# Two preparing stages move into the programs of the attentions behind them

## The reference

```
x = L0_attn_a_hidden_states                     # (8, 512, 128)
x = x + slot_attention(layernorm(x))
x = x + experts(layernorm(x))                   # base_w, lora_A, lora_B, router, top 2 of 8
x = x + polar_attention(layernorm(x))           # 16 heads of 8
x = x + experts(layernorm(x))
x = x + distance_attention(layernorm(x))
x = x + squared_relu_ffn(layernorm(x))
x = x + gated_attention(layernorm(x))
x = x + squared_relu_ffn(layernorm(x))
```

```
q_embed = stack([q_mag * cos(qp), q_mag * sin(qp)]);  k_embed = stack([k_mag * cos(kp), k_mag * sin(kp)])
attn = softmax(einsum(q_embed, k_embed) / D ** 0.5);  out = attn @ v @ wo.T
```

```
G = -(j - P) ** 2 * 2.0 / Z ** 2
probs = softmax(q @ k / sqrt(D) + G);  out = probs @ v @ wo + bo
```

## Time and profile before

| what | value |
|---|---|
| median of 3 runs | 1889.18 us |
| the profiled execution | 1887.09 us |
| its span in the profile | 1885.3 us |
| TensorE (PE) busy | 1622.4 us, 86% |
| VectorE (DVE) busy | 1251.8 us, 66% |
| ScalarE (ACT) busy | 1294.3 us, 69% |
| GpSimd (POOL) busy | 349.0 us, 19% |
| mean granted clock of TensorE | 0.92 |

### The profile page before, as it was taken

The page is one execution under the profiler, slowest core; times in us unless marked ns, Lnnn a source line. Parts: engine busy times, 40 slices in busy tenths (PEclk is TensorE's granted clock), DMA queues, the critical chain, the costliest instruction groups (busy, mean ns, idle before and its releaser), DMA issues. The chain is left out here.

```text
span 1885.3 us, 39080 instructions
## 1 busy us (share of the span) xinstructions
PE 1622.4 (86%) x14558; PEld 779.6 (41%) x14558; DVE 1251.8 (66%) x2538; ACT 1294.3 (69%) x2190; POOL 349.0 (19%) x634
## 2 busy tenths in 40 slices
PE   7899976762999999976789999777764999999988
PEld 4666754640233333346533333344430333333356
DVE  4777776896999999946410010145656999999833
ACT  4556542882688888864579999656662888888863
POOL 3424221441000000014300000023321000000153
PEclk9999995985899999997989999899975999999999
DMA  4000000046222222200131111002233112212101
GB/s 120 1 1 1 1 1 1 10 139 170 64 76 73 81 73 73 67 2 4 40 92 60 58 58 58 3 17 60 82 90 90 56 56 61 63 56 63 35 7 40
DMA packets 114624, 99.04 MB, mean 53 GB/s; under 512 B 25866, under 2 KB 104516, under 8 KB 114436
## 3 DMA queue, kind: packets, MB, share of 16 engines
q1 hardware_dynamic: 112636, 95.61, 17.4%
q10 hardware_dynamic: 1800, 0.92, 0.2%
HBM read 64.34 MB, written 32.11 MB: 51 GB/s over the span
## 5 line engine op out<-in xcount | busy, mean ns | idle before, releaser
L1551 ACT ACTIVATE m_probs<-m_psum 128x512 f32<-128x512 f32 (+1 forms) x768 | 513.7, 758 | 120.1 <-PE m_psum L1459 118.7
L1551 ACT ACTIVATE e_probs<-e_psum 128x512 f32<-128x512 f32 x512 | 277.3, 597 | 82.9 <-PE e_psum L1459 81.6
L1594 DVE TENSOR_REDUCE a_minus_max<-e_psum 128x1 f32<-128x512 f32 x512 | 317.1, 682 | 12.7 <-PE e_psum L1468 5.3
L1594 DVE TENSOR_REDUCE a_minus_max<-m_psum 128x1 f32<-128x512 f32 x512 | 317.0, 682 | 11.7 <-PE m_psum L1468 4.5
L1459 PE MATMUL m_psum<-m_q_stack,m_k_stack 114*32 114x512 bf16 (+1 forms) x4096 | 296.7, 385 | 10.5 <-DMA m_k_stack<-n_parts 8.4
L1479 PE MATMUL m_psum<-m_probs,m_v_ones 128*32 128x512 f32 x2048 | 272.7, 601 | 2.2 <-ACT m_probs L1551 1.4
L1459 PEld LDWEIGHTS m_psum<-m_q_stack,m_k_stack 114*32 114x32 bf16 (+1 forms) x4096 | 105.2, 96 | 211.4 <-issue 113.3
L1459 PE MATMUL e_psum<-e_q_stack,e_k_stack 126*32 126x512 bf16 x2048 | 160.2, 385 | 2.1 <-ACT e_probs L1551 2.1
L1468 PE MATMUL m_psum<-m_k_stack,m_q_stack 48*128 48x512 bf16 x512 | 112.5, 401 | 35.0 <-DMA m_k_stack<-polar_k 34.3
L1468 PE MATMUL e_psum<-e_k_stack,e_q_stack 60*128 60x512 bf16 x512 | 112.6, 401 | 31.6 <-DMA e_q_stack<-gate_parts 31.0
L1479 PE MATMUL e_psum<-e_probs,e_v_ones 128*32 128x512 f32 x1024 | 135.3, 596 | 0.9 <-ACT e_probs L1551 0.8
(11 more groups left out here) (394 smaller groups left out, 2751.3 us busy)
## 6 DMA issues: line engine op xcount, KB each, us to landing
polar_q<-d_p_q_parts SPq DMA_DIRECT2D x24, 256.0 KB, 3.0
polar_k<-d_p_k_parts SPq DMA_DIRECT2D x24, 256.0 KB, 3.1
m_q_stack<-polar_q SPq DMA_DIRECT2D x64, 96.0 KB
m_q_stack<-dist_parts SPq DMA_DIRECT2D x192, 32.0 KB
m_k_stack<-dist_parts SPq DMA_DIRECT2D x192, 32.0 KB
gate_parts<-d_p_curve_parts SPq DMA_DIRECT2D x24, 256.0 KB, 3.0
m_k_stack<-polar_k SPq DMA_DIRECT2D x62, 96.0 KB
e_q_stack<-gate_parts SPq DMA_DIRECT2D x64, 72.0 KB
```

The source lines that it names most:

```text
L1551: act.activation(self.buf.probs[(NT * m + c) % self.buf.PROBS][:, self.WIDE * part:self.WIDE * (part + 1), :], self.ps_s[i % self.PAIRS], ...
L1594: dve.tensor_reduce(self.minus_max[n % 2][:, k:k + 1], ps[:, :], AX.X, ALU.max, negate=True).then_inc(self.bank_free, 1)
```

## The change

The polar stage becomes the class `PolarPhase` and the gated stage the class `GatedPhase`; their steps are called from the streams of `middle_group` and `last_group`, ahead of the attention, and the two programs of their own are gone. So that both fit, the stage's memory lies in the attention's: a helper `Pieces` cuts tensors out of others. Of the polar stage, the normalisation and the experts lie in the buffers `ctxT`, `v_ones` and `probs`, soft and mag in stacks 2 and 3, and the embeddings in `ctx`; the parts lie in a tensor `late`, which the stage behind the attention uses again. The PSUM banks are those of the group. Where an engine takes over a piece, it waits for `early_done` or `all_done` of the stage, and at a bank for `bank_done`.

The attention's beginning is spread over the stage's last steps. Stacks 0 and 1 are filled in polar steps 6 and 7 and loaded behind the stores of blocks 1 and 2, and stacks 2 and 3 are filled behind the stage and loaded behind its last store. In the gated stage stacks 0 and 1 are filled and loaded in steps 7 and 8, and stacks 2 and 3 in step 10. The key stacks of the polar attention are filled by GpSimd. TensorE goes on with the attention's step 0 behind its last stage step (`TAIL`), and VectorE takes the maxima of unit 0 in four chunks (`vector_chunk`) in the last stage steps. In the gated stage the temporaries ez, th and dist lie in the curve tensor itself.

The diff, cut to its core:

```diff
+class Pieces:
...
+    def alloc_sbuf_tensor(self, name, shape, dtype):
+        size = math.prod(shape[1:]) * (2 if dtype == BF16 else 4) // 4
+        room = -(-size // 8) * 8
+        i = next(i for i, region in enumerate(self.regions) if self.used[i] + room <= region.shape[1])
+        piece = self.regions[i][0:shape[0], self.used[i]:self.used[i] + size]
+        self.used[i] += room
+        if dtype != F32:
+            piece = piece.bitcast(dtype)
+        names = "abcd"[:len(shape) - 1]
+        return piece.rearrange(f"p ({' '.join(names)}) -> p {' '.join(names)}", **dict(zip(names, shape[1:])))
...
-        self.soft = [sb(f"{tag}_soft{u}", [P, 2, T], F32) for u in range(2)]
-        self.mag = [sb(f"{tag}_mag{u}", [P, 2, T], F32) for u in range(2)]
-        self.embed = [[sb(f"{tag}_{n}_embed{u}", [P, 2, T], F32) for u in range(2)] for n in "qk"]
+        self.soft = [middle.alloc_sbuf_tensor(f"{tag}_soft{u}", [P, 2, T], F32) for u in range(2)]
+        self.mag = [middle.alloc_sbuf_tensor(f"{tag}_mag{u}", [P, 2, T], F32) for u in range(2)]
+        self.embed = [[context.alloc_sbuf_tensor(f"{tag}_{n}_embed{u}", [P, 2, T], F32) for u in range(2)] for n in "qk"]
...
-        act.activation(self.ez[b % 2][:, :], self.banks.of("z")[:, :], ACT.Exp, scale=-1.0).then_inc(self.ez_ready, 1)
+        wait_ge(act, self.c_split.rest_ready, b - 1)
+        steep = self.curve[b % 2][:, 2, :]
+        act.activation(steep, self.banks.of("z")[:, :], ACT.Exp, scale=-1.0).then_inc(self.ez_ready, 1)
         act.wait_ge(self.ez_ready, b + 1)
         act.wait_ge(self.consts_ready, 1)
-        wait_ge(act, self.c_split.rest_ready, b - 1)
-        act.activation(self.curve[b % 2][:, 2, :], self.ez[b % 2][:, :], ACT.Square, bias=self.consts[:, 1:2], scale=self.SHARP).then_inc(self.steep_ready, 1)
+        act.activation(steep, steep, ACT.Square, bias=self.consts[:, 1:2], scale=self.SHARP).then_inc(self.steep_ready, 1)
...
-        curve, dist = self.curve[b % 2], self.dist[b % 2]
+        curve = self.curve[b % 2]
...
-        dve.tensor_tensor(curve[:, 1, :], dist[:, :], curve[:, 2, :], ALU.mult).then_inc(self.slope_ready, 1)
+        dve.tensor_tensor(curve[:, 1, :], curve[:, 0, :], curve[:, 2, :], ALU.mult).then_inc(self.slope_ready, 1)
         dve.wait_ge(self.slope_ready, b + 1)
-        dve.tensor_tensor(curve[:, 0, :], dist[:, :], curve[:, 1, :], ALU.mult).then_inc(self.curve_ready, 1)
+        dve.tensor_tensor(curve[:, 0, :], curve[:, 0, :], curve[:, 1, :], ALU.mult).then_inc(self.curve_ready, 1)
...
+    def early_done(self, eng):
+        for i in range(2):
+            eng.wait_ge(self.prep.embed_ready[i], NB)
+        eng.wait_ge(self.prep.v_done, NB)
+        eng.wait_ge(self.prep.v_ready, NB)
...
+    def early_done(self, eng):
+        eng.wait_ge(self.prep.p_done, NB)
+        eng.wait_ge(self.prep.v_done, NB)
+        eng.wait_ge(self.prep.k_split.lo_ready, NB)
...
+    def late_pieces(self):
+        return [t[:, :] for t in self.ctxT] + [t[:, :, :, :].rearrange("p t h c -> p (t h c)") for t in self.v_ones] \
+            + [t[:, :, :].rearrange("p h t -> p (h t)") for t in self.probs]
+
+    def stack_pieces(self):
+        return [t[u][:, :, :].rearrange("p h t -> p (h t)").bitcast(F32) for u in range(2, self.SLOTS) for t in (self.q_stack, self.k_stack)]
...
-    def load(self, sp, n, queries=True, keys=True):
+    def load(self, sp, n):
         b, g = divmod(n, NG)
         sp.wait_ge(self.filled[g], self.FILLS)
         wait_ge(sp, self.scores_done, self.UNITS * (n - self.buf.SLOTS + 1))
-        parts = self.loads(b, g, self.buf.q_stack[g], self.buf.k_stack[g])
-        for wanted, part in zip((queries, keys), parts):
-            if wanted:
-                for src, dst in part:
-                    sp.dma_start(dst, src).then_inc(self.loaded[g], 16)
+        for part in self.loads(b, g, self.buf.q_stack[g], self.buf.k_stack[g]):
+            for src, dst in part:
+                sp.dma_start(dst, src).then_inc(self.loaded[g], 16)
 
...
-    def sync(self, sp, skip=0, keys_from=0):
-
+    def sync(self, sp, skip):
+
+        if self.with_max:
+            for n in range(2, skip):
+                self.max_to_stack(sp, n - 2)
         for n in range(skip, self.N):
-            if self.before is not None and n % NG == 0:
+            if n % NG == 0:
                 self.before.parts_stored(sp, n // NG)
-            self.load(sp, n, keys=n >= keys_from)
-            if self.with_max and n >= 2:
+            self.load(sp, n)
+            if self.with_max:
...
+    def fill_key(self, eng, u):
+        k = self.buf.k_stack[u]
+        if self.fixed is not None:
+            last = eng.tensor_copy(k[0:self.rows, 0:GH:2, :], self.fixed[0:self.rows, 0, :].unsqueeze(1).to_broadcast([self.rows, GH // 2, T]))
+        elif self.with_max:
+            eng.wait_ge(self.filled[u], 1)
+            eng.memset(k[32:64, :, :].bitcast(F32), 0.0).then_inc(self.zeroed, 1)
+            eng.wait_ge(self.zeroed, u + 1)
+            last = eng.memset(k[96:self.rows, :, :].bitcast(F32), self.ONES)
...
+    def vector_chunk(self, dve, s, c):
+        if self.with_max and s < self.N:
+            for k in range(4 * c, 4 * c + 4):
+                self.reduce_tile(dve, s, k)
...
+        late = nc.alloc_sbuf_tensor("m_late", [P, 15744], F32)
+        context = Pieces(nc, [sv.ctx[:, :, :].rearrange("p t d -> p (t d)")])
+        polar = PolarPhase(nc, sv, "d3", Pieces(nc, buf.late_pieces()), Pieces(nc, buf.stack_pieces()), context, Pieces(nc, [late[:, :]]), psum)
+        first = Attention(nc, sv, "a3", buf, psum, ((0, 1, 2), 3, (4, 5, 6, 7)), l0b_loads(sv), first=6 * DH, second=6 * DH, before=polar)
...
+        TAIL = NB + 4
+        FILLS = range(6, 8)
 
         with nc.Block() as block:
             @block.sync
             def _(sp):
-                first.sync(sp, keys_from=1)
+                for b in range(NB):
+                    polar.store(sp, b)
+                    if b == 1:
+                        polar.parts_stored(sp, 0)
+                    if 1 <= b <= 2:
+                        first.load(sp, b - 1)
+                first.load(sp, 2)
+                first.load(sp, 3)
+                first.sync(sp, skip=NG)
...
-                first.fill_queries(pool)
+                for s in range(polar.STEPS):
+                    polar.gpsimd(pool, s)
+                    if s in FILLS:
+                        first.fill_query(pool, s - FILLS[0])
+                        first.fill_key(pool, s - FILLS[0])
+                polar.early_done(pool)
+                for u in range(2, NG):
+                    first.fill_query(pool, u)
+                    first.fill_key(pool, u)
                 buf.set_up(pool)
...
-                for s in range(N + first.LAG):
+                polar.vector_start(dve)
+                for s in range(polar.STEPS):
+                    polar.vector(dve, s)
+                    if s == TAIL + 2:
+                        first.zero(dve)
+                    if s >= TAIL + 2 and s - TAIL - 2 < NT:
+                        first.vector_chunk(dve, 0, s - TAIL - 2)
+                polar.early_done(dve)
+                for s in range(1, N + first.LAG):
...
+        late = nc.alloc_sbuf_tensor("e_late", [P, 16128], F32)
+        early = Pieces(nc, buf.late_pieces()[0:4] + buf.stack_pieces() + [sv.pope_table[:, :, :].rearrange("p c t -> p (c t)")] + buf.late_pieces()[4:7])
+        gated = GatedPhase(nc, sv, "d7", sv.l1a_wo[:, :], early, Pieces(nc, [late[:, :]]), psum)
...
+        TAIL = NB + 2
+        FILLS = {NB - 1: (0,), NB: (1,), NB + 2: (2, 3)}
 
         with nc.Block() as block:
             @block.sync
             def _(sp):
-                attention.sync(sp, keys_from=1)
+                for s in range(gated.STEPS):
+                    gated.store(sp, s)
+                    if s == NB - 1:
+                        gated.parts_stored(sp, 0)
+                    for u in FILLS.get(s, ()):
+                        attention.load(sp, u)
+                attention.sync(sp, skip=NG)
                 for b in range(NB):
...
-                for s in range(N + attention.LAG):
+                gated.vector_start(dve)
+                for s in range(gated.STEPS):
+                    gated.vector(dve, s)
+                    if s == NB + 2:
+                        gated.early_done(dve)
+                    for u in FILLS.get(s, ()):
+                        attention.fill_key(dve, u)
+                    if s == TAIL:
+                        attention.zero(dve)
+                        attention.vector_chunk(dve, 0, 0)
+                        attention.vector_chunk(dve, 0, 1)
+                for c in range(2, NT):
+                    attention.vector_chunk(dve, 0, c)
+                for s in range(1, N + attention.LAG):
                     attention.vector(dve, s)
+                    if s == N:
...
-    polar_phase(nc, sv, "d3")
     middle_group(nc, sv)
```

(1 more changed line is left out.)

694 lines of the change are left out of this document (362 added, 332 removed).

## The result

The changed kernel takes 1861.11 us, the median of 4 runs (1858.68 to 1862.63), against 1888.76 us of the kernel before (4 runs beside it, 1886.36 to 1891.96): ratio 0.9848, 95% interval 0.983 to 0.9865. The forecast was 1863.3. The profiled execution is the one of 1858.68 us, span 1856.8.

The account below looks back on a forecast made before the run. TensorE bounds the dense attentions; the two seams before them, last held by SyncE's queue, can shrink. 12.6 + 14.3 - 1.0 = 25.9 us off 1887.09 gives 1861.2; with 2.09 for the median, 1863.3 us; range 1854 to 1875.

Parts of the forecast that it names:

- The queue was last at both seams: Before both attentions, SyncE's queue sets step 2, later than VectorE: by 5.7 us after polar, 1.6 after gated.
- rival A: Queue not last; both steps 2 start by VectorE's path, 34.2 us earlier in all, 1855.0 us; chance 0.14.
- VectorE's path: Step 2 if VectorE alone set it: 461.4 after polar (gain 18.3 us), 1442.2 after gated (gain 15.9).
- Seam 1, SyncE's path: Polar stage to its attention: last store, loads 2 and 3, then rows; step 2 at 467.1, gain 12.6 us.
- Seam 2: Gated stage to its attention: curve stores and loads, then rows; step 2 at 1443.8 by the queue, gain 14.3 us.
- The fills: Stack fills inside polar steps 6, 7 and gated steps 7, 8: 1.0 us taken as cost, between 0 and 8.
- The chunks "earn nothing as such": Unit 0's maxima among the last polar operations: VectorE has no idle time to hide them; the gain is its 18.8 us waiting.
- Rival D: Slower: TensorE's clock stays at 0.5 on into the attention; 1902 us after four such steps; chance 0.04.
- Rival B: About half the gain: steady polar and gated steps get longer; gain 12 us, 1877 us; chance 0.16.
- Rival C: Loads or fills released so late that a wait of equal length replaces the seam; gain within 4 us, 1889; chance 0.04.
- the forecast's own range: Whole kernel: the row landing at both ends and 0 to 8 us for the fills, about 1859 to 1872 us.
- The row's landing: Landing of unit 0's row DMA before step 2: 1.7 us, bounds 0 to 3.7, within 3.3 for the rows.

Follow-up runs that it names:

- e1: Changed kernel with the rows of unit 0's maxima sent ahead of load 3 (polar seam) and ahead of the last curve store (gated seam): 1855.54 us.
- e5: Changed kernel with unit 0's rows sent earlier on SyncE's queue and all chunks of its maxima behind the stages' last steps: 1857.66 us.
- The repeated trace: The changed kernel run again with no edit, in two later sessions: 1868.48 and 1863.43 us.
- e8: Changed kernel with each stack load issuing the DMAs of the keys ahead of those of the queries: 1868.84 us.
- e2: Changed kernel with all four chunks of unit 0's maxima behind each stage's last step, SyncE's order kept: 1860.73 us.
- e4: Changed kernel with the polar stage back in a program of its own, only the gated stage joined to its attention: 1871.21 us.
- e7: Changed kernel with chunks of unit 0's maxima in VectorE's waits, the others last, and rows sent behind load 2: 1852.17 us, again 1849.44.

## Why the prediction was right, and where its sum was off

**The mechanism held.** The queue was last at both seams, as the forecast said against rival A, and e1 shows it by moving two DMAs. VectorE's path, the second limit, lay where the sum had it: 31.9 us behind the last magnitude, 31.88 in e5; at seam 2, 1442.2 - 1410.24 = 32.0, measured 31.1. Rival A is refuted as a description of this kernel; its price was right to within 1 us per seam, and e5 reaches it.

**Seam 1, SyncE's path: 12.6 predicted, 10.3 measured.** This term was 2.3 too large. The repeated trace has its last magnitude at 429.54, as before, so its times compare directly with the sum. SyncE and TensorE in it:

```profile
451.81 1.85 SPq L940 DMA_DIRECT2D polar_k<-m_late  x3
453.70 3.71 SPq L1464 DMA_DIRECT2D m_q_stack<-polar_q  x6
457.46 2.78 SPq L1464 DMA_DIRECT2D m_k_stack<-polar_k  x6
...
465.91 0.43 SPq L1469 DMA_DIRECT2D a_max_dram<-a_max_rows  x1
467.79 0.24 SPq L1471 DMA_DIRECT2D m_q_stack<-a_max_dram  x1
...
469.34 1.04 PE L1532 MATMUL m_psum<-m_q_stack,m_k_stack 114*32 114x512 bf16 x8 [7.90 <-issue]
```

The last polar_k store ends at 453.66 instead of 452.9 (0.8, the polar_q store ahead of it holds the queue); load 2 ends 6.6 us later instead of 5.5 (1.1, the six DMAs behind the stores, e8); load 3 takes 0.2 more; L1469 to L1471 1.9 instead of 1.4 (0.5; with a free queue it was 1.37); the landing of the row load 1.3 behind the end of its issue instead of 1.7 (-0.4). Together 2.2 in this trace. The prices were taken where the queue was free, or where no stores stood just ahead, and were used for a full queue behind stores.

**Seam 2: 14.3 predicted, 13.3 measured.** Counted from the last curves, the queue came to the rows 1.0 us late: the stores of block 6's curve parts began 0.5 later than before, load 2 took 6.2 instead of 5.85 behind them, load 3 6.0. The rows themselves took the 3.3 of the sum (1426.22 to 1429.51). VectorE's path was 0.8 shorter than mine, because the two fills of the key stack took 1.29 us there and not 2.53, as three in a row had made me expect; 0.4 of the 1.2 us went into a longer wait for ScalarE ahead of them (5.27 instead of 4.83).

**The fills: 1.0 taken, 0 measured in the polar half.** The polar stage is as long as before. For the gated half there are only the traces at equal clock above, so its part of the 1.0 stays open. The six late fills ran from 437.00 to 443 us, four of them wholly or partly beside VectorE's two-input operations (L634 and L449), and took 0.94 to 0.96 each, against 3.62 / 4 = 0.9 in the earlier trace rows; GpSimd in the profile after:

```profile
437.00 0.95 POOL L1491 MEMSET m_q_stack<- 114x1024 f32 x1 [21.18 <-DVE ctx L621]
438.01 0.94 POOL L1630 MEMSET m_k_stack<- 32x1024 f32 x1
...
442.03 0.95 POOL L1632 MEMSET m_k_stack<- 18x1024 f32 x1
```

A memset, which reads nothing, is not held up there, while the operation that reads (L216 in the earlier trace rows, L241 above) takes 1.04 to 1.11 us beside such work and 0.24 elsewhere. The Trainium skill, "SBUF — State Buffer", section "SBUF: two separate sides", says that a VectorE operation with two SBUF inputs shuts out only a GpSimd operation that reads SBUF. Both rows agree with it.

**The chunks "earn nothing as such".** Right for VectorE, wrong for the queue: in front of the last split they cost what they delay the last store, 5.6 us at seam 1 (e2). I had included their delay in the sum but not seen that it was a price of their place.

**The clock: nothing taken, 1.7 us gained.** A seam's dense work begins at a granted clock of 0.50. In the kernel before it came back 7.4 us after step 2 began at seam 1 and 5.2 at seam 2, in the changed one after 4.3 to 5.0 and 4.3 to 4.5. Half of the difference is 1.2 to 1.5 and 0.4 to 0.5 us (an estimate), and the attentions are 1.2 and 0.5 us shorter. Rival D, which expected a clock that stays low longer, gave "about 3 us" for seam 2: that counts from the window's edge at 1460, not from step 2 at 1458.08. What brings the clock back is not shown. In these traces more work just ahead of step 2 did not bring it sooner: at seam 1 it came back after 3.5 to 5.2 us in the eight traces in which TensorE waited right in front of step 2, and after 5.8 to 8.7 us in the five in which it did not (before, e4, e5 and both of e7). At seam 2 the two groups overlap (4.3 to 4.5 and 4.4 to 6.6).

Rival B (1877) fails with the polar stage's length, 112.1 to 113.3 against 112.5, and with the total; a loss of 1 us in the gated steps would not be seen. Rival C fails with the traces of VectorE. The errors are -2.3, -1.0, +1.0 and +1.7, together -0.6: the total was better than its terms, and that is luck. The upper end of the forecast's own range was added up wrongly: 1863.3 + 4.0 + 7.0 is 1874, not 1872.

The row's landing: DMA view of the profile after (issues, size, median time to landing), which answers to the earlier trace rows:

```profile
a_max_dram<-a_max_rows SPq DMA_DIRECT2D x64, 8.0 KB, 1.5
```

The Trainium skill, "DMA: Bandwidth & Descriptors", section "Anatomy of one DMA — SWDGE (gpsimd) path", fits its fixed cost of about 2.0 us to DMAs that GpSimd issues. The forecast named the figure without that condition, and the rows go through SyncE's queue. By it each seam would have come 0.3 us later. In the changed kernel's three traces step 2 began 1.55 to 1.62 us behind the start of the row load's issue, 1.3 to 1.4 behind its end, and the measurement decides.

**What stays open.** Why the gated steps take 205.5 us in some traces, 207.5 in others and 212 in others: the granted clock differs (0.97 and 0.86 in the window above), but no run here makes it dip or keeps it up. Why six DMAs behind stores take 3.7 us. And when the clock comes back behind step 2.

## What to carry to other kernels

When a seam between two programs is closed, ask which in-order queue now holds the one transfer that the next dense stretch waits for, and price it as a full queue, in the order in which it is written; then put that transfer ahead of everything that is needed a step later. Compare traces by distances between instructions that all versions have, not by times since the start: here one trace agreed with the forecast to 0.2 us because it came 2.5 us early to the seam and the sum was 2.3 us short. A piece of work that fills a wait pays only if its own inputs are there earlier than what the wait is for.
